# Adapted mixture-of-experts LoRA layer on one core: the transposes of W and of batch 1's inputs moved from TensorE to VectorE

## The chip, the cores and the metric

One core of a Trainium2 chip runs the whole layer as one program. The metric is the device time of one execution in microseconds (us). Below, PE is TensorE, DVE is VectorE, ACT is ScalarE, POOL is GpSimd and SP is SyncE, which here only starts transfers.

## The reference

Eight batches of 512 tokens with 2048 features go through two residual LoRA steps. The first has one adapter per batch, the second a dense matrix W and eight experts of rank 16, of which each token uses the best two:

```python
# x (8, 512, 2048), A0 (64, 2048, 16), B0 (64, 16, 2048)
x = x + einsum('bnr,bor->bno', einsum('bni,bri->bnr', x, B0[id_b]), A0[id_b])
# W (2048, 2048), Wr (8, 2048), A (8, 16, 2048), B (8, 2048, 16)
base = einsum('btd,od->bto', x, W)
logits = einsum('btd,ed->bte', x, Wr) + 5.0 * one_hot(language_b)
weights = softmax(top2(logits)); gates = scatter(weights)
lora = einsum('bter,bte,eor->bto', einsum('btd,erd->bter', x, A), gates, B)
x = x + base + 2.0 * lora
```

The residual is folded into W: the kernel adds the identity to W's diagonal blocks.

## The kernel before, in words

All matrix work is in float32, and each product is made of three rounded ones: high by high, high by low, low by high (`three_products`, lines 810 to 813; `pair_hi` on ACT writes the high part of a tile of W or of its sums, `pair_lo` on DVE the low part).

**Batch 0** multiplies plainly. Its time is cut into 36 slots (`SLOTS0`): in the four blocks of 512 output features there are eight slots with a tile of W each, 24 products of 512 columns per slot, and a ninth (8, 17, 26, 35) with the 12 products of the gated LoRA part. **Batches 1 to 7** use a scheme of seven products in place of eight on half-size blocks (Strassen, Winograd's form), with 60 slots each of 12 products. Their weight operands are W's blocks and four sums of these. Batch 0 makes them while it multiplies and stores them in DRAM (`t_scr`), and every later batch loads them from there, 512 KB a slot (`pair_load`, L780).

**How W comes in.** W lies in DRAM with the output features as rows, but the products want the input features on the partitions. For each of the 32 tiles g, SP loads 512 KB to `raw` (`first_load`, L674, four transfers, runs of 512 bytes). DVE adds the identity to the 8 diagonal tiles (`add_identity`, L684, two instructions each). PE turns the tile over in two halves of four 128x128 transposes into bank 7 (`w_transpose`, L698), and ACT copies each half out (`w_keep`, L709). Then DVE makes the four sums (`w_sums`, L733 to L738) and POOL stores blocks and sums (`w_store` L747 and L748, `w_sums_store` L753).

**How x comes in.** For batches 0 and 1, SP loads 512 KB tiles in runs of 2 KB, and PE turns them in units of four transposes (`x_transpose`, L322); ACT and DVE copy batch 0's out, ACT alone batch 1's (`x_keep`, L341). For batches 2 to 7, the 128-byte runs are scattered on load so that 32x32 blocks lie where DVE's own block-wise transpose gives the whole result (`x_turn`, L268), and PE has no part in it; a tile takes 16 transfers (L289). ACT and DVE split each unit (`x_hi`, `x_lo`), PE multiplies it with the small matrices (`aux_products`, L387 and L389), and later `delta` (L541) and `adapt` (L548) add the first adapter's part.

**What sets the order.** Each engine runs an order written out by hand (`pe_main`, `dve_main`, and so on), in which the work for coming slots stands between that of the present one; semaphores tie the engines. In slot i of batch 0, PE transposes tile i+3, ACT and DVE split tile i+2, and SP starts the load of tile i+5, which waits until tile i+3 has been turned (`raw` has two places for tiles as they come and two for turned ones). `wh` and `wl` have three places, so the split of tile i+2 waits for the products of slot i-1:

```python
            if g >= RING:
                wait_used(e, g - RING)
            e.copy(pair_split(wh, g), pair_source(g)).then_inc(c_wh, 1)
```

The sums go to `tst` or to part of `ost`, and the next sums to the same place wait until the store from there has landed (`d_ts`). At the end of a block, `first_evacuate` (L847, L849) copies the four PSUM banks to `ost`, and the first product of the next block waits for it. Before slot 0 there is a start (`pe_start`, `dve_start`) that turns batch 0's x, the adapters and experts, and tiles 0 to 2.

## Time and profile before

| | us |
|---|---|
| median of 3 runs | 1611.66 |
| lowest, highest | 1604.69, 1611.77 |
| the profiled execution | 1614.29 |
| its span, first to last instruction | 1612.5 |
| PE, DVE, ACT, POOL busy in it | 1580.2, 1179.3, 754.0, 74.1 |

A profile shows one execution. An engine's busy time counts its instructions alone; matmuls overlap, so the time from the start of one to the start of the next tells what it costs, not its duration. The DMA share is the busy time of packets over that of 16 engines; since packets overlap, it can read over 1.

### The profile page before, as it was taken

What the parts mean: (1) busy time and instruction counts of PE and PEld (TensorE: products, weight loads), DVE (VectorE), ACT (ScalarE), POOL (GpSimd) and SP (SyncE); (2) the same over time, 40 slices, a digit from 0 to 9 for tenths busy, and PEclk for the clock granted to TensorE, in tenths of its full rate; (3) what the DMA queues carried; (4) which work ended last, traced back from release to release, by engine and by line L of the source; (5) the groups of instructions that cost most, each with busy time, mean ns of one, the idle gap of its engine ahead of it and who ended that gap; (6) DMA issues with size and microseconds to landing.
All of it is one profiled execution on the core that took longest, in us unless ns stands there. A gap on an engine that the chain in (4) does not pass through costs nothing.

```text
span 1612.5 us, 21199 instructions
## 1 busy us (share of the span) xinstructions
PE 1580.2 (98%) x7766; PEld 1335.1 (83%) x7766; DVE 1179.3 (73%) x1603; ACT 754.0 (47%) x988; POOL 74.1 (5%) x117
## 2 busy tenths in 40 slices
PE   8899999999999999999999999999999999999998
PEld 7777887788888888888888888888888888888887
DVE  5774444687778876887778976888769877787665
ACT  5544433255444544455444554445544544445443
POOL 1222222100000000000000000000000000000000
PEclk9999999999999999999999999999999999999999
DMA  9888687768797886779876797878977797565664
GB/s 250 245 248 248 190 246 211 194 196 229 200 226 232 219 208 206 233 216 237 204 220 222 216 231 188 233 228 225 215 204 230 219 229 198 200 235 201 208 222 157
DMA packets 375658, 351.45 MB, mean 218 GB/s; under 512 B 250554, under 2 KB 294890, under 8 KB 374634
## 3 DMA queue, kind: packets, MB, share of 16 engines
q1 hardware_dynamic: 366290, 318.62, 71.6%
q0 software_dynamic: 8992, 30.94, 6.0%
q8 instruction: 62, 1.02, 0.3%
q10 hardware_dynamic: 272, 0.52, 0.1%
q14 instruction: 42, 0.34, 0.1%
HBM read 280.75 MB, written 68.82 MB: 217 GB/s over the span
## 4 chain that ended last, share of the span: by engine, by line
PE 93%; DMA 4%; DVE 1%; SPq 1%; issue 1%; ACT 1%; POOL 0%; ACTq 0%; DVEq 0%
PE pb L811 27%; PE pb L812 27%; PE pb L813 27%; PE pb L387 4%; PE pb L389 3%; PE pb L541 2%; PE pb L698 1%; DMA raw<-in_L_cond_W_dram 1%; DMA b0n<-in_L_cond_B_dram 1%; DMA ost<-in_L_cond_B_dram 1%; DMA t_scr<-raw 1%; PE pb L322 0%; SPq L674 0%; DMA ost<-in_x_dram 0%; SPq L1356 0%
## 5 line engine op out<-in xcount | busy, mean ns | idle before, releaser
L807 DVE TENSOR_TENSOR wl<-raw,wh 128x1024 fp32r<-128x1024 f32 (+1 forms) x456 | 555.0, 1217 | 349.3 <-ACT wh L803 349.0
L803 ACT CAST wh<-raw 128x1024 fp32r<-128x1024 f32 (+1 forms) x456 | 477.1, 1046 | 680.1 <-PE pb L813 680.0
L811 PE MATMUL pb<-wh,sh 128*128 128x512 f32 x1568 | 612.8, 391 | 0.5 <-DVE ost L849 0.5
L812 PE MATMUL pb<-wl,sh 128*128 128x512 f32 x1568 | 611.5, 390 | 0.0
L813 PE MATMUL pb<-wh,sl 128*128 128x512 f32 x1568 | 611.1, 390 | 0.0
L813 PEld LDWEIGHTS pb<-wh,sl 128*128 128x128 f32 x1568 | 294.3, 188 | 62.8
L811 PEld LDWEIGHTS pb<-wh,sh 128*128 128x128 f32 x1568 | 294.6, 188 | 56.1 <-DVE wl L807 0.9
L812 PEld LDWEIGHTS pb<-wl,sh 128*128 128x128 f32 x1568 | 294.6, 188 | 55.0
L387 PE MATMUL pb<-awb,xah 128*128 128x304 f32 x512 | 139.2, 305 | 0.0
L389 PE MATMUL pb<-awb,xal 128*128 128x256 f32 x512 | 135.0, 281 | 0.0
L811 PE MATMUL pb<-wh,xh 128*128 128x512 f32 x256 | 106.1, 415 | 0.8 <-DVE ost L849 0.8
L813 PE MATMUL pb<-wh,xl 128*128 128x512 f32 x256 | 102.0, 398 | 0.0
L812 PE MATMUL pb<-wl,xh 128*128 128x512 f32 x256 | 101.8, 398 | 0.0
L389 PEld LDWEIGHTS pb<-awb,xal 128*128 128x128 f32 x512 | 96.9, 189 | 4.2
L387 PEld LDWEIGHTS pb<-awb,xah 128*128 128x128 f32 x512 | 96.7, 189 | 4.4
L620 DVE TENSOR_TENSOR sl<-pool_a,sh 128x512 fp32r<-128x512 f32 x120 | 82.0, 684 | 0.0
L709 ACT COPY raw<-pb 128x512 f32<-128x512 f32 x64 | 37.7, 589 | 77.1 <-PE pb L698 74.7
L615 ACT CAST sh<-pool_a 128x512 fp32r<-128x512 f32 x120 | 73.5, 613 | 0.0
L548 DVE TENSOR_TENSOR pool_a<-pool_a,pb 128x512 f32<-128x512 f32 x88 | 58.8, 680 | 7.9 <-PE pb L541 7.9
L364 DVE TENSOR_TENSOR xal<-pool_a,xah 128x512 fp32r<-128x512 f32 x88 | 60.2, 685 | 5.8 <-ACT xah L359 5.6
L359 ACT CAST xah<-pool_a 128x512 fp32r<-128x512 f32 x88 | 54.7, 623 | 14.0 <-DVE pool_a L268 13.8
L813 PEld LDWEIGHTS pb<-wh,xl 128*128 128x128 f32 x256 | 48.9, 191 | 10.9
(151 smaller groups left out, 1335.0 us busy)
## 6 DMA issues: line engine op xcount, KB each, us to landing
raw<-t_scr SPq DMA_DIRECT2D x392, 512.0 KB, 4.2
xst<-in_x_dram SPq DMA_DIRECT2D x768, 32.0 KB, 3.9
raw<-in_L_cond_W_dram SPq DMA_DIRECT2D x124, 128.0 KB, 4.0
raw<-bt_scr SPq DMA_DIRECT2D x28, 512.0 KB, 3.6
out_dram<-ost SPq DMA_DIRECT2D x28, 512.0 KB, 4.2
out_dram<-u SPq DMA_DIRECT2D x28, 512.0 KB, 3.4
t_scr<-tst POOLq DMA_DIRECT2D x17, 512.0 KB, 5.2
t_scr<-raw POOLq DMA_DIRECT2D x32, 256.0 KB, 4.8
```

The costliest lines, as they stand in the source:

```text
L359: e.copy(x_high(n, u).rearrange("p k t -> p (k t)"), two(n, q, kp)).then_inc(c_xh, 1)
L364: e.tensor_tensor(out=x_low(n, u).rearrange("p k t -> p (k t)"), in0=two(n, q, kp), in1=x_high(n, u).rearrange("p k t -> p (k t)").bitcast ...
L387: e.matmul(pb[:, aux_bank(n, u // 8) + t, 0:2 * AW], x_high(n, u)[:, k, toks], cols[:, 0:2 * AW], start=u % 8 == 0 and k == 0, stop=False)
L389: last = e.matmul(pb[:, aux_bank(n, u // 8) + t, 0:LOW], x_low(n, u)[:, k, toks], cols[:, 0:LOW], start=False, stop=u % 8 == 7 and k == 1)
L548: e.tensor_tensor(out=two(n, q, kp), in0=two(n, q, kp), in1=pb[:, delta_bank(n, u), :], op=ALU.add)\
L615: e.copy(sh[:, h % SR, :, :].rearrange("p k t -> p (k t)"), two(b, SUM_QUARTER[product], kp)).then_inc(c_sph, 1)
L620: e.tensor_tensor(out=sl[:, h % SR, :, :].rearrange("p k t -> p (k t)"), in0=two(b, SUM_QUARTER[product], kp), in1=sh[:, h % SR, :, :].rea ...
L803: e.copy(pair_split(wh, g), pair_source(g)).then_inc(c_wh, 1)
L807: e.tensor_tensor(out=pair_split(wl, g), in0=pair_source(g), in1=pair_split(wh, g).bitcast(f32), op=ALU.subtract).then_inc(c_wl, 1)
L811: e.matmul(o, h, wh[:, g % RING, k, :], start=start, stop=False)
L812: e.matmul(o, h, wl[:, g % RING, k, :], start=False, stop=False)
L813: return e.matmul(o, l, wh[:, g % RING, k, :], start=False, stop=stop)
```

## The change

The outputs of the seven-product scheme are no longer the left and the right half of the features: within each block of 512 output features, the first and the second 256 are the two halves, and for the inputs the even and the odd features. A run in DRAM is then 64 floats (256 bytes) for x of batches 1 to 7 and for W. Both are scattered on load and turned by DVE with instructions of 128x512 whose input has a step of two elements:

```diff
-        x_b = x.rearrange("b (h v j) (c k a i) -> b h c k a j v i", h=2, j=32, c=4, k=4, a=4)
+        x_b = x.rearrange("b (h v j) (c k a n) -> b h c k a j v n", h=2, j=32, c=4, k=2, a=4)
...
-            e.transpose(two(n, q, kp).rearrange("p (k v j) -> p v k j", k=2, v=8),
-                        x_block(m)[:, :, u % 2 * 2:u % 2 * 2 + 2, :]).then_inc(c_xc, 1)
+            e.transpose(two(n, q, kp).rearrange("p (g j) -> p g j", g=16),
+                        x_block(m).rearrange("p (g i h) -> p h g i", g=16, h=2)[:, u % 2, :, :]).then_inc(c_xc, 1)
...
         def x_unit(u):
-            return u // 4, u % 4
+            return u // 8 * 2 + u % 2, u // 2 % 4
...
-        raw_w = W.rearrange("(w c j p) (h k n) -> c k w p j h n", w=2, c=4, j=2, p=P, h=2, k=HK)
+        raw_w = W.rearrange("(c g j) (k a n) -> c k a j g n", c=4, g=16, k=HK, a=4)
...
+        def w_turn(e, g):
...
+            diagonal = k // 2 == c
+            raw_landed(e, g)
+            if w >= 2:
+                e.wait_ge(c_wl, g - 2 - (g % 9 < 2) + 1)
+                wait_sums(e, w - 2)
                 e.wait_ge(d_bs[w % 2], 32 * (w // 2))
...
+            for h in range(2):
+                e.transpose(w_kept(g)[:, h, :].rearrange("p (g j) -> p g j", g=16),
+                            w_raw(g).rearrange("p (g i h) -> p h g i", g=16, h=2)[:, h, :, :])\
+                 .then_inc(c_id if diagonal else c_wc, 1)
+            if diagonal:
+                for h in range(2):
+                    e.wait_ge(c_id, 4 * c + 2 * (k % 2) + h + 1)
+                    block = w_kept(g)[:, h, k % 2 * HT:(k % 2 + 1) * HT].rearrange("p (n h) -> p h n", h=2)[:, h, :]
+                    e.tensor_tensor(out=block, in0=block, in1=ident[:, :], op=ALU.add).then_inc(c_wc, 1)
```

`w_transpose`, `w_keep`, `add_identity`, `x_keep` and the calls of `x_transpose` for batch 1 are gone, and with them the bank between PE and ACT. The adapters, Wr and A are read with the same step of two in the start. From the fourth tile of W on, two of the four sums are POOL's:

```diff
+        def w_sum_3(e, g):
+            b11, b12, b21, b22 = w_blocks(g)
+            e.wait_ge(c_wc, 2 * w_number(g) + 2)
+            wait_sum_place(e, g)
+            e.tensor_tensor(out=w_sum(g)[:, 3, :], in0=b12, in1=b11, op=ALU.subtract).then_inc(c_tp, 1)
+
+        def w_sum_2(e, g):
+            b11, b12, b21, b22 = w_blocks(g)
+            e.wait_ge(c_t, 2 * w_number(g) + 8)
+            e.tensor_tensor(out=w_sum(g)[:, 2, :], in0=b21, in1=w_sum(g)[:, 0, :], op=ALU.subtract).then_inc(c_tp, 1)
...
             for i in range(SLOTS0):
-                if i + 2 < SLOTS0 and (i + 2) % 9 != 8:
+                sums = i + 2 < SLOTS0 and (i + 2) % 9 != 8
+                if sums and i:
+                    w_sum_3(e, i + 2)
+                if i + 3 < SLOTS0 and (i + 3) % 9 != 8:
+                    w_store(e, i + 3)
+                if sums and i:
+                    w_sum_2(e, i + 2)
+                if sums:
                     w_sums_store(e, i + 2)
```

The results of batches 1 to 7 go out in runs of 1 KB, two transfers of 256 KB in place of one of 512 KB. In the later batches, x's units stand at slightly other slots, and what follows them (`bx`, `aux_adapted`, `delta`, `adapt`, the gates) three slots later:

```diff
-                e.dma_start(out_v[b, 0, :, :, c * CW:(c + 1) * CW], ost[:, 2 * c:2 * c + 2, :]).then_inc(d_ost[c], 16)
+                for t in range(2):
+                    e.dma_start(out_v[b, 0, t, 0, :, 2 * c:2 * c + 2, :],
+                                ost[:, 2 * c + t, :].rearrange("p (c n) -> p c n", c=2)).then_inc(d_ost[c], 16)
...
-        X_AT = {4 * (u // 2) + 4 + u % 2: u for u in range(16)}
+
+        X_AT = {at: u for u, at in enumerate((4, 5, 8, 9, 12, 13, 16, 17, 21, 24, 25, 28, 29, 32, 33, 36))}
...
-                        if 41 <= i < 57:
-                            delta(e, n, i - 41)
+                        if i >= 44:
+                            delta(e, n, i - 44)
```

On PE, at the border of two slots of batch 0 (`pb` are the PSUM banks, `xst` and `raw` the tiles of x and W as they came), there stood before:

```order
L812 MATMUL pb<-wl,xh 128x512
L813 MATMUL pb<-wh,xl 128x512
L322 MATMUL pb<-ident,xst 128x128 x4
L698 MATMUL pb<-ident,raw 128x128 x4
L811 MATMUL pb<-wh,xh 128x512
```

and stands now:

```order
L809 MATMUL pb<-wl,xh 128x512
L810 MATMUL pb<-wh,xl 128x512
L808 MATMUL pb<-wh,xh 128x512
```

Both rows of transposes went. On DVE, slot 11 of batch 0 was the split of tile 13 (`wl`), the four sums of tile 13 (`tst`) and the low part of a unit of x (`xal`):

```order
L807 TENSOR_TENSOR wl<-raw,wh 128x1024
L733 TENSOR_TENSOR tst<-raw 128x256
L734 TENSOR_TENSOR tst<-raw 128x256
L736 TENSOR_TENSOR tst<-tst,raw 128x256
L738 TENSOR_TENSOR tst<-raw,tst 128x256
L364 TENSOR_TENSOR xal<-pool_a,xah 128x512
```

and is now:

```order
L270 STREAM_TRANSPOSE pool_a<-xst 128x512
L804 TENSOR_TENSOR wl<-raw,wh 128x1024
L674 STREAM_TRANSPOSE raw<-raw 128x512 x2
L349 TENSOR_TENSOR xal<-pool_a,xah 128x512
L717 TENSOR_TENSOR tst<-raw 128x256
L721 TENSOR_TENSOR tst<-tst,raw 128x256
```

Three transposes came, two sums went, and the sums stand behind the turning of the next tile. In the start, DVE made the sums of tile 0 right after `st48`, ahead of the first `adapt`s (`pool_a`):

```order
L414 TENSOR_TENSOR st48<-aux,st48 128x4x16
L733 TENSOR_TENSOR tst<-raw 128x256
L734 TENSOR_TENSOR tst<-raw 128x256
L736 TENSOR_TENSOR tst<-tst,raw 128x256
L738 TENSOR_TENSOR tst<-raw,tst 128x256
L548 TENSOR_TENSOR pool_a<-pool_a,pb 128x512 x2
```

Now tile 1 is turned there, and the sums of tile 0 come after the split of tile 1, directly ahead of tile 2's turning and tile 1's sums:

```order
L804 TENSOR_TENSOR wl<-raw,wh 128x1024
L1138 TENSOR_TENSOR late<-late 128x136
L717 TENSOR_TENSOR tst<-raw 128x256
L719 TENSOR_TENSOR tst<-raw 128x256
L721 TENSOR_TENSOR tst<-tst,raw 128x256
L724 TENSOR_TENSOR tst<-raw,tst 128x256
L674 STREAM_TRANSPOSE raw<-wrn 128x512 x2
L717 TENSOR_TENSOR tst<-raw 128x256
```

## Rows read from the trace of the kernel before

**Rows 1.** the page, busy time of each engine

```profile
PE 1580.2 (98%) x7766; PEld 1335.1 (83%) x7766; DVE 1179.3 (73%) x1603; ACT 754.0 (47%) x988; POOL 74.1 (5%) x117
```

**Rows 2.** windows: us, busy (count) of PE PEld DVE ACT POOL, clock, DMA share, GB/s

```profile
63.08:131.66 68.58, 63.90 (x326) 52.38 (x325) 45.78 (x104) 30.66 (x47) 18.69 (x28) 0.97 0.78 228
131.66:199.24 67.58, 66.46 (x368) 57.08 (x369) 29.22 (x54) 28.20 (x48) 16.81 (x26) 1.00 0.75 216
199.24:265.61 66.37, 65.62 (x360) 56.15 (x361) 29.26 (x57) 25.58 (x44) 14.94 (x24) 1.00 0.74 213
265.61:329.47 63.86, 57.60 (x279) 47.98 (x278) 37.17 (x87) 18.43 (x28) 12.13 (x19) 0.95 0.76 208
329.47:1600.00 1270.53, 1270.53 (x6042) 1068.78 (x6043) 996.72 (x1238) 614.31 (x764) 0.00 (x0) 1.00 0.78 218
```

**Rows 3.** PE's order of time in slot 14 of batch 0 (start, us)

```profile
176.52 0.60 PE L698 MATMUL pb<-ident,raw 128*128 128x128 f32 x4
176.88 0.48 PE L811 MATMUL pb<-wh,xh 128*128 128x512 f32 x1
177.19 0.40 PE L812 MATMUL pb<-wl,xh 128*128 128x512 f32 x1
177.42 0.39 PE L813 MATMUL pb<-wh,xl 128*128 128x512 f32 x1
```

**Rows 4.** PE's order of time at its two long stops

```profile
62.31 1.12 PE L698 MATMUL pb<-ident,wrn 128*128 128x128 f32 x4 [6.42 <-ACT raw L709]
...
284.68 1.11 PE L698 MATMUL pb<-ident,raw 128*128 128x128 f32 x4 [5.75 <-DMA raw<-in_L_cond_W_dram]
286.02 0.63 PE L812 MATMUL pb<-wl,xh 128*128 128x512 f32 x1
286.45 0.63 PE L813 MATMUL pb<-wh,xl 128*128 128x512 f32 x1
```

**Rows 5.** DVE's groups (xcount | busy, mean ns | idle before, releaser)

```profile
L807 DVE TENSOR_TENSOR wl<-raw,wh 128x1024 fp32r<-128x1024 f32 x452 | 552.2, 1222 | 342.7 <-ACT wh L803 342.4
...
L364 DVE TENSOR_TENSOR xal<-pool_a,xah 128x512 fp32r<-128x512 f32 x88 | 60.2, 685 | 5.8 <-ACT xah L359 5.6
L268 DVE STREAM_TRANSPOSE pool_a<-xst 128x512 f32<-128x512 f32 x56 | 39.4, 704 | 0.0
...
L684 DVE TENSOR_TENSOR raw<-raw,ident 128x128 f32<-128x128 f32 x16 | 3.9, 287 | 15.5 <-DMA raw<-in_L_cond_W_dram 15.5
```

**Rows 6.** ACT's groups: two copies of 512 elements

```profile
L709 ACT COPY raw<-pb 128x512 f32<-128x512 f32 x64 | 37.7, 589 | 77.1 <-PE pb L698 74.7 <-DMA t_scr<-raw 2.5
...
L1075 ACT COPY a0t<-pb 128x512 f32<-128x512 f32 x4 | 4.3, 1079 | 0.7 <-PE pb L1070 0.7
```

**Rows 7.** POOL's and DVE's order of time around 50 us

```profile
50.46 1.62 POOL L1304 COPY xst<-ost 128x256 f32<-128x256 f32 x4 [18.47 <-DMA ost<-in_L_cond_B_dram]
...
51.20 0.62 DVE L733 TENSOR_TENSOR tst<-raw 128x256 f32<-128x256 f32 x1
...
64.06 0.43 DVE L733 TENSOR_TENSOR tst<-raw 128x256 f32<-128x256 f32 x1 [3.75 <-ACT raw L709]
```

**Rows 8.** the page, DMA issues, last number: us to landing

```profile
t_scr<-tst POOLq DMA_DIRECT2D x17, 512.0 KB, 5.2
```

**Rows 9.** DMA packets of 1440 to 1560, 460 to 580, 131.6 to 199.2 us

```profile
DMA packets 7429, 25.25 MB, mean 210 GB/s; under 512 B 768, under 2 KB 768, under 8 KB 7422
...
q1 hardware_dynamic: 7422, 25.16, 61.4%
...
DMA packets 32606, 27.49 MB, mean 229 GB/s; under 512 B 25695, under 2 KB 25695, under 8 KB 32599
...
q1 hardware_dynamic: 32599, 27.39, 83.6%
...
DMA packets 13093, 14.56 MB, mean 215 GB/s; under 512 B 1040, under 2 KB 10512, under 8 KB 13087
```

**Rows 10.** a window in which the DMA share reads over 1

```profile
205.00:210.00 5.00, 5.00 (x28) 4.22 (x27) 2.31 (x5) 2.54 (x4) 0.89 (x2) 1.00 1.08 316
```

More of the change, by code:

```diff
@@ L328, in x_keep_act @@
             e.wait_ge(c_tr, u + 1)
-            e.copy(two(0, q, kp), pb[:, x_bank(0, u), :]).then_inc(c_x0[0], 1)
+            e.copy(two(0, q, kp), pb[:, x_bank(u), :]).then_inc(c_x0[0], 1)
         def x_keep_dve(e, u):
@@ L671, in first_load @@
                      .then_inc(landed, 16)
-                else:
-                    for h in range(2):
-                        e.dma_start(w_raw(g)[:, 2 * w:2 * w + 2, h, :], raw_w[c, k, w, :, :, h, :])\
-                         .then_inc(landed, 16)
-        def add_identity(e, g):
-            c, k = divmod(g, 9)
-            if k // 2 != c:
-                return
-            raw_landed(e, g)
-            for h in range(2):
-                block = w_raw(g)[:, 2 * h + k % 2, h, :]
-                e.tensor_tensor(out=block, in0=block, in1=ident[:, :], op=ALU.add).then_inc(c_id, 1)
@@ L686, in w_transpose @@
[L686 removed]
+            else:
+                for a in range(4):
+                    e.dma_start(w_raw(g)[32 * a:32 * a + 32, :].rearrange("p (g n) -> p g n", g=16), raw_w[c, k, a])\
+                     .then_inc(landed, 16)
+        def w_turn(e, g):
             c, k = divmod(g, 9)
             w = w_number(g)
[L689 to L699 removed]
@@ L996, in a_transpose @@
             for k in range(4):
-                last = e.transpose(pb[:, m, k * P:(k + 1) * P], an[:, (4 * m + k) * P:(4 * m + k + 1) * P], ident[:, :])
+                last = e.transpose(pb[:, m, k * P:(k + 1) * P], tile_of(an[:, :], a_tiles(m).start + k), ident[:, :])
             last.then_inc(c_ap, 1)
@@ L1272, in dve_start @@
             bx_lo(e, 0)
-            w_sums(e, 0)
+            w_turn(e, 1)
             for u in range(2):
@@ L1284, in dve_start @@
             g_lo(e)
+            w_sums(e, 0)
+            w_turn(e, 2)
             w_sums(e, 1)
[L1286 to L1287 removed]
         def pool_start(e):
@@ L1376, in pe_main @@
             for i in range(SLOTS0):
-                more = i + 3 < SLOTS0 and (i + 3) % 9 != 8
                 if i == 4:
@@ L1442, in act_main @@
             for i in range(SLOTS0):
-                more = i + 3 < SLOTS0 and (i + 3) % 9 != 8
-                if i < 2:
-                    w_keep(e, i + 2, 1)
                 if i == 6:
@@ L1474, in act_main @@
                         sum_hi(e, 1, 0, kp)
-                if i and more:
-                    w_keep(e, i + 3, 1)
                 if i in (17, 25):
@@ L1527, in dve_main @@
                         adapt(e, 1, u)
+                if i + 3 < SLOTS0 and (i + 3) % 9 != 8:
+                    w_turn(e, i + 3)
+                if 9 <= i < 25:
+                    x_lo(e, 1, i - 9)
                 if i + 2 < SLOTS0 and (i + 2) % 9 != 8:
```

285 lines of the change are left out of this document (122 added, 163 removed).

## The prediction, made before the changed kernel had run

> **What bounds the kernel now.** I read the engines' busy time first: PE is busy for 1580.2 of 1612.5 us, DVE for 1179.3 [rows 1]. The average hides two kinds of time, so next I read windows. Batches 1 to 7 (329.47 to 1600 us) have PE busy for every microsecond of 1270.53 at full clock [rows 2]. The change takes no PE instruction out of them, so nothing can be won there; it can only be lost. Batch 0 takes four windows of 68.58, 67.58, 66.37 and 63.86 us (slots 0 to 8, 9 to 17, 18 to 26, 27 to 35), with PE idle for 4.68, 1.12, 0.75 and 6.26 us of them. So in the two middle windows PE has nearly no gaps, and what it does less is won unless something else takes over; in the first and the last, waits count too. PE's own order of time gives the price of a transpose group and the two long stops [rows 3, 4]. DVE's groups give what the new work costs there [rows 5], and the DMA packets tell how much room the transfers have [rows 9].
>
> **PE: transposes removed.** A group of four starts 0.36 us before the next product, and this product takes 0.31 us to its successor where 0.23 is the rule: 0.36 + 0.08 = 0.44 us [rows 3]. The 64 half tiles of W and 16 units of batch 1's x are 80 groups, 35.2 us. Six groups lie ahead of the first product at 63.08 us, where other things bound; 74 remain. In slots 9 to 17 there are 16 of W and 9 of x, 25 x 0.44 = 11.0 us; in slots 18 to 26 16 and 7, 10.1 us; in slots 27 to 35 10 of W, 4.4 us; the other 16, 7.0 us, are in slots 0 to 8.
>
> **PE: waits removed.** At 278.9 us PE stops for 5.75 us because the transposes of a tile stand in its queue and the tile has not come [rows 4]. Now DVE waits for the tile, and PE needs it two slots later, some 10 us of slack. I let this stop go, and with it the slow clock behind it: products 0.43 us apart in place of 0.23 [rows 4], and a mean clock of 0.95 in that window [rows 2], which is 5% of 63.86, 3 us, of which the stop itself holds a part; I take 2. The other stop, 6.42 us at 55.9 us [rows 4], waited for ACT's copy of tile 2, which waited for a store. This chain goes too, but the start has others (below).
>
> **ACT** loses 80 copies of 0.589 us [rows 6], 47 us of an engine that is busy for 754.0 [rows 1]. Nothing waits for ACT for long in batch 0's middle, so I take nothing for it.
>
> **DVE: what comes.** A tile costs two transposes. The nearest row is the same instruction without the step of two, 0.704 us [rows 5]. From below nothing speaks for less. From above, ACT's copy of 512 elements costs 0.589 us packed and 1.079 us with a stepped output [rows 6], 1.83 times; by this a transpose would be 1.29 us. I take 0.70, the nearest row: the same operation, engine and size. In slots 9 to 24 DVE then has per slot: `pair_lo` 1.22, three transposes 2.11, the low part of x 0.69 and two sums of 0.43 [rows 5, 7], 4.9 us, and in two tiles of eight twice 0.29 more for the identity. The 67.58 us of slots 9 to 17 are eight slots and a half one, 7.95 us each; with three groups less, PE's slot lasts 6.6. DVE fits, with 1.7 us over, and its split of a tile is needed two slots later. So this is hidden, as long as a transpose stays under some 1.1 us.
>
> **POOL's sums.** Two of 256 elements per slot, on an engine busy for 74.1 us in all [rows 1]; hidden behind everything, except that they may slow DVE. The trace shows that: DVE's first sum of 256 elements took 0.62 us while POOL copied, and 0.43 us otherwise [rows 7]. So a DVE sum or split beside each of POOL's loses 0.2 us, 0.4 per slot, inside the 1.7 us. The Trainium skill, SBUF — State Buffer, section "Who interferes with whom", says that a VectorE instruction with two SBUF inputs contends with a GpSimd one that reads SBUF, and that the second blocks until the first ends. By that rule the loss could be up to the length of POOL's own instruction, which no row shows; from POOL's copy (1.62 us for four, [rows 7]) I bound it at twice 0.8 per slot for a form with two inputs, 1.6 us, which would just use up the room.
>
> **DMA: smaller packets.** Between 1440 and 1560 us (no x is loaded) q1 moves 25.16 MB in 7422 packets with 61.4% of 16 engines, 1179 engine-us or 46.9 us per MB. Between 460 and 580 us it moves 27.39 MB in 32599 packets with 83.6%, 1605 engine-us. The 2.23 MB more are worth 105, so 321 engine-us are for 25177 small packets more: 12.8 ns each [rows 9]. A tile of W had 1024 packets and gets 2048; a tile of batch 1's x had 256 and gets 2048. For slots 9 to 17 (8.5 tiles of W, 3.5 of x) that is 15000 packets, 192 engine-us, on top of 0.75 x 16 x 67.58 = 811 [rows 2]: 1003, or 62.7 us at a share of 1. The share can read over 1: 1.08 at 316 GB/s [rows 10], by which it is 58. PE alone would need 67.58 - 11.0 = 56.6. So in this window DMA and PE come out nearly even, and I take 59.5, 8 us less than before. For slots 18 to 26 (8 of W, 2.5 of x) it is 786 + 162 = 948, 59.3 or 54.9 us, against 56.3 of PE: I take 58, 8.4 less. In slots 27 to 35, 7 tiles of W add 7168 packets, but the first two tiles of batch 2's x lose 4096, and 777 + 39 = 816 engine-us is 51 us: no bound. The bounds of a packet's price are nothing (packets of 256 bytes pack better than those of 128) and 25.6 ns (one costs as much as two of 128). The Trainium skill, DMA: Bandwidth & Descriptors, section Specifications, asks for at least 512 bytes for the full rate and says that smaller transfers do read-modify-write; W's runs go from just that size to half of it, so it speaks against this change. What it would do here is the second rival.
>
> **The last quarter.** 4.4 us of transposes, 5.75 of the stop and 2 of the clock are 12.2; but there DVE has three `adapt`s a slot, the top-two chain and a turning, and the evacuation behind slot 26 now stands behind a turning of 1.4 us. I give 2 back: 10 less.
>
> **The start and slots 0 to 8.** Slots 0 to 6 are DVE's: `adapt` and split of two units, the split of the tile, now also its turning (1.4) for two sums less (0.86), so 0.5 us a slot more. Further, the sums of tile 0 come later, and those of tile 1 wait for their store to land, 5.2 us [rows 8], in front of tile 2's split, where PE will stop in slot 1. On the other side, the stop of 6.42 us goes, slot 0 can begin some 5 us earlier, and the waits of transposes for tiles 10 and 11 go. Adding the DVE instructions up one by one I come to a start of slot 9 at 127.7 us in place of 131.66: 4 less, give or take 5. This is the softest term.
>
> **Later batches.** x's units and `delta` move by up to three slots, in an order in which PE has no gap; x loads have half the packets (98304 less, 1258 engine-us, or 79 us of share over 1270); results go out in 112 transfers for 56. PE bounds: 0. If this cover went, one DVE round late would show as PE idle in a window that has none now. The last store starts as two transfers: +0.3.
>
> **Sum:** -4 - 8 - 8.4 - 10 + 0.3 = -30. The profiled execution took 1614.29 us (span 1612.5 and 1.8 around it) and would take 1584. The median of the runs, 1611.66, is 2.6 below it, so the forecast of the median is 1582 us.
>
> **The rivals.**
> - PE alone bounds: packets of 256 bytes cost little more than their bytes. Then the middle windows give 11.0 and 10.1 and the last 12.2: -37, 1575 us. For it speaks that PE is gapless there; against it the share of 0.75 before any packet was added. 0.15.
> - DMA bounds at the full 12.8 ns and a share of 1: middle windows 62.7 and 59.3, -4.9 and -7.1, last -8, start -4: -24, 1588. 0.21. This is also the skill's rule in its mild form.
> - The same at 25.6 ns: 811 + 384 = 1195 engine-us are 74.7 us in place of 67.6, the second window 786 + 325 are 69.4 (+3), the start loses its 4, the last keeps -8: about +2, 1614, no change. 0.05.
> - The softest term fails: in slots 0 to 6 DVE's chain and the wait for the store cost 8 instead of winning 4, all else as forecast: -18, 1594. 0.07.
> - **Slower:** DVE becomes the bound of batch 0. At 1.29 us a transpose, DVE's slot is 6.7, with 0.4 for POOL 7.1: under the old 7.95, but slots 0 to 6 lose 12 and the last quarter is even; the whole comes out near zero. Each 0.1 us more costs 80 x 0.1 = 8 us. At 1.6 us it is +25, 1637. It decides from 1.3 us. For it speaks ACT's stepped row; against it that this is another engine, and output, not input. 0.04.
>
> **How the numbers follow.** The forecast case has 0.48. Half a percent, 8 us, is about what a measurement of this kernel can tell from no change. Faster by more than that are the forecast, the first, the second and the fourth rival: 0.48 + 0.15 + 0.21 + 0.07 = 0.91; no change 0.05; slower 0.04. The range goes from 1571 (the first rival with a start that gives 4 more) to 1596 (the fourth, and the second with a start that gives nothing), which leaves out the third and the fifth and some of the edges.
>
> **What would show it.** Right: no transposes of W on PE; slots 10 to 16 between 6.5 and 6.9 us apart; the stop before slot 29 gone; `w_turn` transposes near 0.70 us; batches 1 to 7 unchanged with PE gapless; the DMA share in the middle windows from 0.9 to 1.05. Wrong: transposes over 1 us, DVE busy for over 90% of a middle window, PE waiting for `wl` while DVE waits for W, or slot 9 starting after 131.66 us.

## The result, and the profile after

| | before | after |
|---|---|---|
| median, 15 runs each on one chip | 1609.90 | 1603.86 |
| lowest, highest | 1602.12, 1611.77 | 1601.00, 1606.35 |
| profiled execution | 1614.29 | 1606.35 |
| its span | 1612.5 | 1604.6 |

The ratio is 0.9966, 95% interval [0.9955, 0.9978]: faster, by 6 us and not by 30. That is less than the half percent (8 us) which the prediction took for what can be told from no change, though the interval leaves 1 out, and it lies outside the range of 1571 to 1596 us.

The stretches of the profiled executions in us, cut at the first product of a slot (read off PE's order of time), each with the part of the forecast's sum that spoke of it:

| stretch | before | after | forecast | came |
|---|---|---|---|---|
| start of slot 9 | 131.66 | 141.51 | -4 | **+9.85** |
| slots 9 to 26 | 133.95 | 122.61 | -16.4 | -11.34 |
| slots 27 to 35 | 63.86 | 55.18 | -10 | -8.68 |
| batches 1 to 7 | 1278.43 | 1280.52 | 0 | +2.09 |
| behind the last product | 4.6 | 4.8 | +0.3 | +0.2 |

The page of the changed kernel, busy time of each engine, beside [rows 1]:

```profile
PE 1556.7 (97%) x7446; PEld 1308.1 (82%) x7446; DVE 1221.7 (76%) x1625; ACT 713.9 (44%) x908; POOL 126.2 (8%) x176
```

Its windows by block, beside [rows 2] (us, busy of PE, PEld, DVE, ACT, POOL, clock, DMA share, GB/s):

```profile
58.01:141.51 83.50, 57.67 (x252) 46.10 (x253) 60.65 (x117) 24.10 (x33) 35.16 (x45) 0.87 0.89 215
141.51:203.00 61.49, 57.71 (x269) 48.51 (x269) 41.23 (x65) 15.51 (x22) 28.75 (x39) 0.94 0.96 229
203.00:264.12 61.12, 58.34 (x272) 48.84 (x273) 38.81 (x64) 14.55 (x22) 28.68 (x40) 0.95 0.93 235
264.12:319.30 55.18, 54.32 (x240) 44.52 (x241) 43.43 (x85) 12.87 (x18) 22.84 (x30) 0.94 0.92 238
319.30:1599.80 1280.50, 1280.46 (x6076) 1074.34 (x6076) 999.93 (x1239) 615.23 (x764) 0.00 (x0) 1.00 0.72 216
```

PE's work shrank as the transposes went (57.67 us in the first block in place of 63.90), but the first block grew by 15 us: PE is idle for 26 of its 83.50 us, DVE is busy for 60.65 in place of 45.78, and the granted clock is 0.87 in place of 0.97. (Slot 0 starts 5.07 us earlier, at 58.01, so that slot 9 is later by 9.85 only.) What PE waits for, whole run (us in total, times, longest):

```profile
PE pb L808 <- DVE ost L846: 14.9, 4, 9.9
PE pb L1147 <- ACT bt L1152: 9.9, 1, 9.9
PE pb L408 <- DVE st L399: 5.1, 2, 3.0
PE pb L526 <- DVE pool_a L533: 4.0, 3, 2.7
```

The two longest are the stops to read. **The stop in slot 1.** DVE's order of time, changed kernel:

```profile
63.17 0.42 DVE L724 TENSOR_TENSOR tst<-raw,tst 128x256 f32<-128x256 f32 x1
63.80 1.30 DVE L674 STREAM_TRANSPOSE raw<-wrn 128x512 f32<-128x512 f32 x2 [0.20 <-DVE tst L724]
68.70 0.42 DVE L717 TENSOR_TENSOR tst<-raw 128x256 f32<-128x256 f32 x1 [3.60 <-DMA t_scr<-tst]
...
71.31 1.28 DVE L533 TENSOR_TENSOR pool_a<-pool_a,pb 128x512 f32<-128x512 f32 x2
72.67 1.29 DVE L553 TENSOR_TENSOR xl<-pool_a,xh 128x512 fp32r<-128x512 f32 x2
73.88 1.30 DVE L674 STREAM_TRANSPOSE raw<-raw 128x512 f32<-128x512 f32 x2
```

ACT's, and PE's, behind it:

```profile
75.22 1.04 ACT L800 CAST wh<-raw 128x1024 fp32r<-128x1024 f32 x1 [1.98 <-DVE raw L674]
76.17 1.03 ACT L1152 COPY bt<-pb 128x512 f32<-128x512 f32 x1
```

```profile
77.25 1.11 PE L1147 MATMUL pb<-ident,xst 128*128 128x128 f32 x4 [9.86 <-ACT bt L1152]
...
79.01 0.63 PE L808 MATMUL pb<-wh,xh 128*128 128x512 f32 x1
79.44 0.63 PE L809 MATMUL pb<-wl,xh 128*128 128x512 f32 x1
```

Read backwards: PE stops for a copy on ACT; this stands behind the high part of tile 3, which waits for tile 3's turning at 73.88, and that is late because DVE, in order, had waited 3.60 us for the store of tile 0's sums to leave `tst`. None of the waiting engines was short of work to do; a queue held it. And behind the stop products are 0.43 us apart: the granted clock is 0.50 from 79 to 82 us, 1.00 before the stop (66 to 68 us).

**The stop ahead of slot 9.** POOL's order of time, then DVE's and PE's:

```profile
127.43 0.73 POOL L744 DMA_DIRECT2D t_scr<-raw  x1 [4.74 <-DVE raw L674]
...
128.75 1.80 POOL L735 TENSOR_TENSOR ost<-raw,ost 128x256 f32<-128x256 f32 x1
131.09 0.78 POOL L750 DMA_DIRECT2D t_scr<-ost  x1 [0.54 <-POOL ost L735]
```

```profile
125.82 1.30 DVE L674 STREAM_TRANSPOSE raw<-raw 128x512 f32<-128x512 f32 x2 [1.78 <-DMA raw<-in_L_cond_W_dram]
...
133.35 1.30 DVE L674 STREAM_TRANSPOSE raw<-raw 128x512 f32<-128x512 f32 x2 [3.40 <-DMA raw<-in_L_cond_W_dram]
...
140.67 1.29 DVE L846 COPY ost<-pb 128x512 f32<-128x512 f32 x2 [4.85 <-DMA t_scr<-ost]
```

```profile
141.51 0.76 PE L808 MATMUL pb<-wh,xh 128*128 128x512 f32 x1 [9.87 <-DVE ost L846]
142.07 0.63 PE L809 MATMUL pb<-wl,xh 128*128 128x512 f32 x1
```

PE may not write the banks again until they are copied to `ost`; the copy waits until the sums that lie in `ost` have been stored; POOL issued this store at 131.09 only, since the store of tile 10, which had to be turned first, stands ahead in its queue and its own sum took 1.80 us; and it landed 9.5 us later, against a median of 5.5 for `tst`. Smaller stops of this kind stand ahead of slots 18 (3.8 us) and 27 (0.7 us).

### The profile page after: what moved, and what is told of

The parts are those of the page before. It is cut to its first block, busy times and chain, and to the rows that moved or that the text cites. A ratio compares the mean times of both kernels' runs of the same rounds, so it can differ in the third digit from the quotient of the medians.

```text
span 1604.6 us, 20300 instructions
## 1 busy us (share of the span) xinstructions
PE 1556.7 (97%) x7446; PEld 1308.1 (82%) x7446; DVE 1221.7 (76%) x1625; ACT 713.9 (44%) x908; POOL 126.2 (8%) x176
## 4 chain that ended last, share of the span: by engine, by line
PE 88%; DVE 5%; DMA 4%; ACT 1%; issue 1%; SPq 1%; POOL 0%; DVEq 0%; ACTq 0%; POOLq 0%
PE pb L808 26%; PE pb L809 26%; PE pb L810 26%; PE pb L372 4%; PE pb L374 3%; PE pb L526 2%; DMA xst<-in_x_dram 1%; DVE raw L674 1%; DMA t_scr<-ost 1%; DVE wl L804 1%; DMA b0n<-in_L_cond_B_dram 1%; ACT wh L800 1%; DVE pool_a L533 1%; SPq L659 0%; DMA an<-in_L_cond_A_dram 0%
## 5 line engine op out<-in xcount | busy, mean ns | idle before, releaser
L808 PEld LDWEIGHTS pb<-wh,xh 128*128 128x128 f32 x256 | 50.7, 198 | 27.3 <-issue 16.1
L270 DVE STREAM_TRANSPOSE pool_a<-xst 128x512 f32<-128x512 f32 x72 | 50.9, 706 | 14.0 <-DMA xst<-in_x_dram 13.9
```

The lines of the kernel that those rows point to most:

```text
L808: e.matmul(o, h, wh[:, g % RING, k, :], start=start, stop=False)
```

## The experiments

All ratios are to the kernel before, run beside each in five rounds; intervals are 95%. Gains of an edit are told as differences of medians. They are uncertain by some 2 us: the kernel before measured 1611.0 us beside e1, e2, e6 and e7 and 1609.9 beside the changed kernel, so that by the ratios each of these gains about 2 us more. For an edit's mechanism the traces decide, but each shows one execution: in those of the kernels built on the changed one, slot 0 starts between 56.62 and 58.55 us, so a stretch counted from slot 0 says more than a time. A slot's length is the distance from its first product to the next slot's.

| run | edit, on the changed kernel unless said | median | ratio |
|---|---|---|---|
| after | | 1603.86 | 0.9966 [0.9955, 0.9978] |
| e1_pool_order | sums' store ahead of W's | 1600.43 | 0.9932 [0.9912, 0.9951] |
| e2_sums0_early | tile 0's sums early | 1602.07 | 0.9938 [0.9920, 0.9957] |
| e6_ost_swap | evacuation swapped | 1603.97 | 0.9953 [0.9936, 0.9970] |
| e7_three | e1 + e2 + e6 + x load order | 1597.44 | 0.9918 [0.9899, 0.9937] |
| e3_sums_dve | no sums on POOL | 1595.09 | 0.9915 [0.9901, 0.9928] |
| e5_shift_before | before + the shift of three slots | 1613.07 | 1.0015 [1.0000, 1.0029] |
| e8_x_whole | e7 + x tiles loaded whole | 1592.12 | 0.9898 [0.9883, 0.9913] |
| e9_bt_first | e7 + ACT's order | 1598.74 | 0.9943 [0.9929, 0.9958] |
| e12_pool_idle_sums | e3 + unused sums on POOL | 1601.17 | 0.9944 [0.9926, 0.9963] |
| e10_all_dve | e3 + e1 + e2 + both x edits | 1592.58 | 0.9895 [0.9877, 0.9913] |
| e13_all_dve_swap | e10 + e6 | 1590.36 | **0.9883 [0.9863, 0.9903]** |
| e14_half_turn | e13, tiles half turned | 1589.14 | 0.9857 [0.9840, 0.9873] |

**POOL's order.** Move W's store back behind the sums':

```diff
-                if i + 3 < SLOTS0 and (i + 3) % 9 != 8:
-                    w_store(e, i + 3)
                 if sums and i:
                     w_sum_2(e, i + 2)
                 if sums:
                     w_sums_store(e, i + 2)
+                if i + 3 < SLOTS0 and (i + 3) % 9 != 8:
+                    w_store(e, i + 3)
```

> The changed kernel with one edit on GpSimd: in a slot of batch 0 the store of W's plain blocks (w_store of tile i+3, which waits for the transposes of that tile) stands again behind the last sum and the store of the sums of tile i+2, as before the change. Theory Q (queue order: the store of tile 9's sums was issued at 131.09 us, behind that wait, and landed at 140.58; the first evacuation waited for it): slot 9 starts near 134 instead of 141.51, TensorE's 9.9 us wait for the evacuation is 2 to 4 us, and the time is 6 to 10 us below the changed kernel's 1603.9, 1594 to 1598 (ratio to the kernel before 0.990 to 0.993). Rival D (the transfers themselves are late, since 256-byte packets fill the DMA engines, share 0.89 to 0.96 in batch 0): the store still lands 9 us after its issue and slot 9 starts within 2 us of 141.5, 1602 to 1604 (ratio 0.996). Rival P (POOL has no room before its sum is ready, so the order does not matter): as D, with the store of the sums issued at 129 or later.

The time fell by 3.4 us, about half of the least that the theory wanted; slot 9 starts at 138.34, not near 134. The store went out at 129.12 in place of 131.09, and landed only at 137.5, 8.4 us later. So the queue's order is part of it, and the long landing, rival D's, the other part. Rival P was not far off either: POOL's sum could not begin before DVE's was ready, at 127.86 in place of 128.75, and 1.1 of the 2.0 us that the store gained are this sum's own length, 0.72 us in place of 1.80.

**Tile 0's sums** before tile 1's turning, in `dve_start`:

```diff
             bx_lo(e, 0)
+            w_sums(e, 0)
             w_turn(e, 1)
...
             g_lo(e)
-            w_sums(e, 0)
             w_turn(e, 2)
```

> The changed kernel with one edit on VectorE: the sums of W's tile 0 are made right behind the first half of bx, as before the change, ahead of tile 1's transposes instead of behind them. Theory V (VectorE's queue: its first sum of tile 1 waited 3.60 us, to 68.70, for the store of tile 0's sums to leave the staging tile; this wait went on through pair_lo, adapt, w_turn(3), ScalarE's pair_hi(3) and its copy of Bt to TensorE's 9.86 us stop at 67.4 to 77.3): slot 2 starts at 77 to 80 instead of 83.74 and the time is 4 to 7 us below 1603.9, 1597 to 1600 (ratio 0.993 to 0.994). Rival W (what is late is W's tile 3 or the transposes themselves, 0.7 us each, and the wait for the store only fills that time): slot 2 at 82 to 84, time within 1.5 us of 1603.9. Rival S (what slot 1 gains is lost at slot 8, whose stop ends with the store of tile 9's sums, whatever came earlier): slot 2 early, slot 9 again at 140 to 141.5, time within 2 us of 1603.9.

Slot 2 starts at 81.84, 1.9 us earlier, and the median is 1.8 lower. Most of PE's stop (8.5 of 9.9 us) stays, but this does not clear the wait for the store: the edit did not take it away. POOL's and DVE's order of time in this run:

```profile
56.97 0.75 POOL L750 DMA_DIRECT2D t_scr<-tst  x1
...
67.07 0.43 DVE L717 TENSOR_TENSOR tst<-raw 128x256 f32<-128x256 f32 x1 [4.02 <-DMA t_scr<-tst]
```

Tile 0's sums were made by 51.9 us, but POOL issued their store at 56.97, behind its own copies, and DVE still waited 4.02 us for it (3.60 before): it had landed 10.1 us after its issue, in the changed kernel 4.8 us after (63.90 to 68.70). The landing moved by 1.6 us, and about that is what the run gained. Were the wait gone, DVE could turn tile 3 some 4 us earlier (an estimate from this row); the other half of the stop would remain. No run took the wait away. Slot 9 kept the gain (139.48), against the third theory.

**The evacuation** to the halves of `ost` that hold no sums first:

```diff
+            o = (t + 2) % 4
             if c:
-                e.wait_ge(d_ost[t // 2], 32 * c)
-            if t < 2:
+                e.wait_ge(d_ost[o // 2], 32 * c)
+            if o < 2:
...
-                e.copy(ost[:, t, :], pb[:, t, :]).then_inc(c_eva, 1)
+                e.copy(ost[:, o, :], pb[:, t, :]).then_inc(c_eva, 1)
```

> The changed kernel with one edit in the evacuations of batch 0: banks 0 and 1 go to the two output tiles that hold no sums of W, banks 2 and 3 to the two that also stage the sums, so that the first two evacuations need not wait for the store of the sums. Theory E (the stops ahead of slots 9, 18 and 27, 9.9, 3.8 and about 1 us, are waits for the staging tile and not for the evacuation's work): TensorE's waits for the evacuation are under 2 us in all, the half clock behind them is gone or shorter (2.8 us each), and the time is 10 to 18 us below 1603.9, 1586 to 1594 (ratio 0.985 to 0.990). Rival H (VectorE's and ScalarE's queues are themselves behind, since VectorE waits for x and W there; the evacuation would be late without the staging tile): the stop ahead of slot 9 is 4 us or more, and the time 1598 to 1602 (ratio 0.993 to 0.995).

A miss: the same median within 0.1 us, outside both ranges (2 us less by the ratios). Slot 9 starts at 137.27 in place of 141.51, but takes 11.65 us in place of 8.29, as PE now stops inside it for the second pair of banks, whose copies wait 4.0 and 8.4 us for the same store. The wait was moved behind two banks, not removed. Later the profile is ahead all the same, at slot 32 by 5.0 us (291.89 for 296.93), since slot 27 takes 5.96 us in place of 8.82; but in slot 32 PE waits 2.1 us for an `adapt` of DVE, and slots 32 and 33 give 3.4 us back (8.86 and 7.77 for 7.05 and 6.21).

**The three together, and the second x load** of batch 1 a slot later:

```diff
-                if i in (4, 5):
-                    x_load(e, 1, i - 4)
+                if i in (4, 6):
+                    x_load(e, 1, i // 2 - 2)
```

> The changed kernel with four edits together: the store of W's plain blocks behind the sums on GpSimd, the sums of tile 0 early on VectorE, the second load of batch 1's x issued behind first_load(11) instead of ahead of it, and banks 0 and 1 evacuated to the tiles that hold no sums. Theory (the changed kernel lost what it saves on TensorE in waits of three queues): slot 2 at 77 to 80, slot 9 at 124 to 128, slot 18 at 185 to 190, slot 27 at 246 to 250, batch 1 from 302 to 307, and 1583 to 1590 (ratio 0.983 to 0.988). Rival (the DMA engines, at a share of 0.93 to 0.96 in the middle of batch 0, have nothing left to give, so that whatever starts earlier waits longer for its W and x): slots 9 to 36 take 5 us or more longer than the changed kernel's 177.8 us, and the time is 1593 to 1600.

Up to slot 9 the theory's numbers came, or nearly (79.53, 128.42), and behind it, in part, the rival's: slots 9 to 35 took 181.39 us, 3.6 more than the changed kernel's 177.79, where the rival wanted 5. The time is inside the rival's range. Ahead of slot 18 PE waits 6.5 us. DVE there, in this run:

```profile
185.99 0.42 DVE L721 TENSOR_TENSOR ost<-ost,raw 128x256 f32<-128x256 f32 x1
191.08 0.71 DVE L270 STREAM_TRANSPOSE pool_a<-xst 128x512 f32<-128x512 f32 x1 [4.67 <-DMA xst<-in_x_dram]
191.72 1.18 DVE L804 TENSOR_TENSOR wl<-raw,wh 128x1024 fp32r<-128x1024 f32 x1
...
195.78 1.28 DVE L847 COPY ost<-pb 128x512 f32<-128x512 f32 x2
```

The turning of x, first in the slot, waits 4.67 us for its tile, and the evacuation stands behind it.

**All sums on DVE**; POOL only stores:

```diff
-            if w < 3:
+            if True:
                 e.tensor_tensor(out=t[:, 3, :], in0=b12, in1=b11, op=ALU.subtract).then_inc(c_t, 1)
...
-                if sums and i:
-                    w_sum_3(e, i + 2)
...
-                if sums and i:
-                    w_sum_2(e, i + 2)
```

> The changed kernel with all four sums of W on VectorE and none on GpSimd, so that GpSimd only issues stores again. VectorE gets 0.85 us a slot more (two sums at 0.42), but its operations are no longer prolonged by GpSimd's (wl at 1.55 to 1.76 us instead of 1.22 in slots 3 to 8, xl's pair at 2.04 to 2.37 instead of 1.29), and the store of the sums no longer waits for GpSimd's two sums (0.7 to 1.8 us each) behind W's store. Theory G (the split of the sums is what costs slots 3 to 9): wl back at 1.22, slot 9 starts 4 to 7 us earlier than 141.51, and the time is 1597 to 1600 (ratio to before 0.992 to 0.994). Rival V (VectorE's total work decides, 60.7 of 83.5 us up to slot 9): slot 9 at 141 or later and 1603 to 1608 (ratio 0.996 to 0.999). Slots 10 to 17, where VectorE was busy 29.3 of 45.5 us, should stay at 6.5 us either way.

The largest gain of one edit, 8.8 us (8.2 by the ratios), more than the theory asked; slot 9 starts at 135.00. DVE's order of time with the splits beside POOL's sums in the changed kernel, then the same in this run:

```profile
92.48 1.55 DVE L804 TENSOR_TENSOR wl<-raw,wh 128x1024 fp32r<-128x1024 f32 x1 [0.35 <-ACT wh L800]
...
95.32 2.37 DVE L553 TENSOR_TENSOR xl<-pool_a,xh 128x512 fp32r<-128x512 f32 x2
...
100.72 1.76 DVE L804 TENSOR_TENSOR wl<-raw,wh 128x1024 fp32r<-128x1024 f32 x1
```

```profile
91.74 1.22 DVE L802 TENSOR_TENSOR wl<-raw,wh 128x1024 fp32r<-128x1024 f32 x1
...
94.24 1.29 DVE L553 TENSOR_TENSOR xl<-pool_a,xh 128x512 fp32r<-128x512 f32 x2
...
99.24 1.22 DVE L802 TENSOR_TENSOR wl<-raw,wh 128x1024 fp32r<-128x1024 f32 x1
```

Over slots 2 to 5 the changed kernel's splits of W and x lasted some 3 us longer than this run's. Slots 10 to 16 stayed at 6.5 us, with twice the sums on DVE.

**The same work on POOL, for nobody**: e3_sums_dve with two subtractions a slot on a spare tile.

```diff
+            for half in range(2):
+                e.wait_ge(c_tp, 2 * n + half)
+                e.tensor_tensor(out=spare[:, :], in0=spare[:, :], in1=spare[:, :], op=ALU.subtract)\
+                 .then_inc(c_tp, 1)
```

> The form of e3_sums_dve (all four sums of W on VectorE, 1595.1 us), and GpSimd makes in every slot of batch 0, behind the slot's stores, two 128x256 subtractions on a tile of its own that nobody reads: GpSimd's two sums of the changed kernel again as work, without anyone waiting for their result and without W's stores behind them in the slot. It measures what GpSimd's use of the shared port costs VectorE. Theory C (contention is most of what e3_sums_dve won back, 8.8 us): wl and xl of slots 3 to 8 are prolonged again (wl 1.4 to 1.8 us instead of 1.22), slot 9 starts 3 us or more after e3_sums_dve's 135.99, and the time is 1598 to 1602. Rival O (what e3_sums_dve won is the order: the sums' store no longer waits behind GpSimd's sums and W's store): slot 9 within 1.5 us of 136, and the time 1594 to 1597.

(The 135.99 there is the third product of e3's slot 9; the first, as everywhere in this text, is at 135.00.) The time rose by 6.1 us to 1601.17 (4.7 by the ratios), and the fastest run of this kernel (1596.67) is above the slowest of e3 (1595.61). The time is theory C's, its signs are not: slot 9 came only 1.4 us later or, counted from slot 0, 2.7, and in slots 3 to 8 a single split of a tile was prolonged, at 98.60 us, to 1.73. DVE's splits of tiles and of x between 64 and 305 us, this run, then e3_sums_dve:

```profile
L803 DVE TENSOR_TENSOR wl<-raw,wh 128x1024 fp32r<-128x1024 f32 x31 | 40.6, 1308 | 17.7 <-ACT wh L799 17.7
...
L350 DVE TENSOR_TENSOR xal<-pool_a,xah 128x512 fp32r<-128x512 f32 x16 | 11.4, 710 | 0.0
```

```profile
L802 DVE TENSOR_TENSOR wl<-raw,wh 128x1024 fp32r<-128x1024 f32 x31 | 37.7, 1217 | 23.7 <-ACT wh L798 23.3
...
L349 DVE TENSOR_TENSOR xal<-pool_a,xah 128x512 fp32r<-128x512 f32 x16 | 10.6, 660 | 0.0
```

So work on POOL that nobody waits for costs 5 to 6 of the 8.8 us. How it does is open. DVE's instructions in these two rows are 3.7 us longer, but most of that lies in slots 10 to 16 and 19 to 25, which take 6.5 us in both runs. Counted from slot 0 the profile loses 4.8 us by slot 18, and the two largest parts stand where DVE waits for a load: for W's tile 11 5.0 us, in e3 2.4, and for a tile of x ahead of slot 18 4.2, in e3 2.5. Whether POOL's work made these loads late, or only this execution did, was not tried. What remains of the 8.8, some 3 us, is of the size of e1's 3.4.

**The shift of later batches**, alone in the kernel before; `bx`, `aux_adapted` and the gates move likewise:

```diff
-                        if 41 <= i < 57:
-                            delta(e, n, i - 41)
+                        if i >= 44:
+                            delta(e, n, i - 44)
```

> The kernel before with one part of the change alone: in batches 1 to 7 bx, the adapted aux sum, the deltas and the gates of the next batch stand three slots later. The changed kernel's batches 1 to 7 took 2.3 us more than before's (1285.3 against 1283.0 us, 0.3 us a batch) with TensorE gapless in both; the deltas' matmuls were 0.124 us apart instead of 0.121. Theory L (the shift costs it): batches 1 to 7 take 1285 us, the time is 1 to 3 us above the kernel before (ratio 1.0005 to 1.002). Rival M (it comes with the x transposes as 256-byte packets or the output's stores, that is with other traffic on SBUF, or with the layout of the products' operands): batches 1 to 7 take 1283.0 within 0.3 us, and no difference can be measured.

Its batches 1 to 7 took 1280.5 us, as the changed kernel's, in place of 1278.4, PE gapless; this window is the evidence, since the ratio's interval just reaches 1:

```profile
321.03:1601.50 1280.47, 1280.44 (x6076) 1074.50 (x6076) 999.14 (x1239) 615.15 (x764) 0.00 (x0) 1.00 0.79 216
```

All 12 other profiles of kernels with the shift say the same: from the first product of batch 1 to the last of the kernel they take 1279.85 to 1280.25 us, this one 1280.12, and before 1278.04. (The absolute lengths in the expectation, 1283.0 and 1285.3, run to the end of the span; the difference is the same.) The run says one more thing: with the same program up to batch 1 as before, it starts slot 0 at 58.83 us and slot 9 at 125.53, where the profiled execution of before had 63.08 and 131.66. Part of what that profile showed in its start was that execution's own.

**x loaded whole**, on e7:

```diff
-                if 11 <= i < 23:
-                    x_load(e, 1, (i - 7) // 2, (0, 1) if i % 2 else (2, 3))
+                if 11 <= i < 23 and i % 2:
+                    x_load(e, 1, (i - 7) // 2)
```

> The four edits of e7_three and a fifth: batch 1's input tiles 2 to 7 are each loaded by eight transfers at once in every second slot of batch 0, instead of four in one slot and four in the next, which SyncE issues only after the W tile in between. Theory X (latency of x decides slots 15 and 17 of e7_three: VectorE's x transposes, first in its slot, waited 2.9, 4.7 and 6.0 us for their tile, and with them W's transposes and the evacuation ahead of slot 18): these waits are under 1 us, slot 15 takes 6.5 instead of 8.38 and slot 17 takes 6.6 to 8 instead of 10.41, and the time is 3 to 6 us below e7_three's 1597.4, 1591 to 1594. Rival B (the DMA engines' throughput decides; what x gains, W loses): VectorE waits for W instead, slots 9 to 27 still take 127 to 128 us, and the time is within 1.5 us of 1597.4.

Theory X: 5.3 us less (3.2 by the ratios), slot 14 (the expectation miscounts it as 15) at 6.49 us in place of 8.38, slot 17 at 8.01 in place of 10.41. The waits for x fell to 1.9 and 2.4 us, if not under 1. A transfer's place in SP's queue, not the DMA engines' capacity, was what x lacked.

**ACT's order**, on e7:

```diff
-                pair_hi(e, i + 2)
                 if i in (1, 2):
                     bt_copy(e, 2 * i - 2)
+                    bt_copy(e, 2 * i - 1)
+                pair_hi(e, i + 2)
```

> The four edits of e7_three and, instead of a fifth on the loads, one on ScalarE: in slots 1 and 2 the copies of Bt's transposes stand ahead of pair_hi of the W tile two slots on. Theory A (TensorE's stop in slot 1, still 7.3 us in e7_three, is a wait for a copy that stands on ScalarE behind pair_hi(3), and this one waits for VectorE's transposes of tile 3 to 71.6 us; nothing that slot 2's products need is late): the stop in slot 1 is under 1.5 us, slot 2 starts at 71 to 74 instead of 79.53, and the time is 4 to 7 us below e7_three's 1597.4, 1590 to 1593. Rival V (VectorE's own queue, busy without a gap from 65 to 80 us, is what slots 3 to 5 wait for): slot 2 early but slot 5 at 99 to 101 as in e7_three (100.79), and the time within 1.5 us of 1597.4.

The rival, and worse: PE's stop is 5.3 us in place of 7.3 and slot 2 starts 1.1 us earlier, but slot 3 takes 8.68 in place of 6.33 us, slot 5 starts at 102.75, and the time is 1.3 us above e7's. DVE's queue was the limit behind ACT's. (Slot 17 was longer too, 12.00 us: DVE could turn its tile of x at 193.41 us only, in e7 at 191.08; why the tile came later is open.)

**Together, sums on DVE:**

> The form of e3_sums_dve with four of the edits tried before: on GpSimd the sums' store ahead of W's store, the sums of tile 0 early on VectorE, batch 1's second input tile loaded behind first_load(11), and its tiles 2 to 7 loaded whole in every second slot. If the gains are of different waits and add up (e3_sums_dve -8.8, e1 -3.4, of which e3 holds part, e2 -1.8, the whole loads -5.3 against the changed kernel or its combination): slot 2 at 79, slot 9 at 127 to 130, slot 18 at 188 to 191, batch 1 from 301 to 304, and 1586 to 1590 (ratio 0.985 to 0.987). Rival (slots 1 to 8 are bound by VectorE's total work, 50 of 62 us, and its four sums cost more there than the contention did): slot 9 at 131 or later and the time 1590 to 1594, no better than e8_x_whole's 1592.1.

The rival's numbers: slot 9 at 132.45, no better than e8. Its reason, that DVE's total work bounds there, is at most a part: ahead of slot 9 DVE stands idle for 3.34 us.

```profile
131.61 1.29 DVE L844 COPY ost<-pb 128x512 f32<-128x512 f32 x2 [3.34 <-DMA t_scr<-ost]
```

The sums' store was issued at 123.78 and landed 7.8 us later, and this kernel lacks the one edit of e8 that lets two banks go ahead of it.

> As e10_all_dve, and banks 0 and 1 evacuated to the output tiles that hold no sums. Theory E (the last stops ahead of slots 9 and 18 are waits for the staging tile): 2 to 4 us below e10_all_dve. Rival H (the evacuation waits for VectorE's own queue, as e6_ost_swap, which won 0.1 us by itself, seemed to say): within 1 us of e10_all_dve, either way.

By the medians theory E, at its low edge: 2.2 us. But the intervals overlap, and in the profiles batch 0 takes 246.09 us from slot 0 in place of 246.80, so that most of the difference between them stands ahead of slot 0, which this edit does not touch; between E and H this is open. The traces do show what the edit does here: the store goes out at 123.97, in e6 at 132.24, the copies of the second pair of banks wait 2.2 and 4.6 us for it in place of 4.0 and 8.4, and slot 9 starts 65.49 us after slot 1 in place of 67.49. This is the best version that computes the whole layer, 1.2% below before and 13.5 us faster than the changed kernel. Its middle windows:

```profile
129.21:191.17 61.96, 56.84 (x268) 47.20 (x269) 44.72 (x81) 17.12 (x23) 16.55 (x26) 0.97 1.07 255
191.17:251.32 60.15, 57.54 (x273) 47.94 (x273) 42.53 (x80) 13.38 (x20) 15.91 (x24) 0.97 1.04 241
```

**Less turning**, on e13. This kernel leaves half of eight tiles of W unturned (the expectation says which), so its output is not the layer's; it only measures:

```diff
             for h in range(2):
+                n = 1 if h and 3 <= g <= 11 else 16
```

> As e13_all_dve_swap, the best so far (1590.4 us, slot 1 at 63.72 and slot 9 at 129.21), with one thing left out: of the two transposes of each of W's tiles 3 to 7 and 9 to 11 on VectorE the second turns 32 columns instead of 512, so that these tiles' second halves keep old values in the output's first batch and in what is stored of W. That takes some 0.6 us out of VectorE's work in each of slots 0 to 8, about 5 us in all, and changes no transfer and no wait. Theory V (up to slot 9 VectorE's own work is the limit, 49.7 us busy of 60.7 with TensorE at 47.7): slot 9 comes 3 to 5 us earlier after slot 1's start (60.5 to 62.5 us instead of 65.5), and the time is 3 to 5 us below 1590.4, 1585 to 1587.5. Rival L (the stops are latency: of transfers, and of hand-overs between the engines, with VectorE's 11 idle us as room): slot 9 within 1.5 us of 65.5 after slot 1, and the time within 1.5 us of 1590.4.

Between the theories: from slot 1 to slot 9 63.16 us in place of 65.49, 2.3 less for 4.2 taken (eight times 0.69 - 0.17). By these two executions DVE's work bounds about half of that stretch, latency the rest. The median is 1.2 us lower, 4.2 by the ratios, which leaves open how much of the 2.3 reaches the end; in the profiled execution slot 10 gave it back (10.62 us in place of 7.87).

## Why the prediction was wrong

**The step that failed** is the term "The start and slots 0 to 8", put at -4, give or take 5, and called the softest: it measured +9.85, 14 of the 22 us that are missing. Slot 0 did begin 5.1 us earlier, as said; slots 0 to 7 took 7.1 us more (70.63 for 63.54), slot 8 with the stop at its end 7.8 more (12.87 for 5.04). Its parts:
- "up one by one I come to a start of slot 9 at 127.7". The instructions' prices were right (transposes 0.686 and 0.706 us for 0.70). The sum counted work and one wait on DVE. That wait came no larger than foreseen: 3.6 us, the store landing 4.8 us after its issue. It left out what DVE's lateness does through the other queues: ACT's copy of Bt behind the high part of tile 3, with 9.9 us of PE standing still, and the half clock behind it (slot 1 took 19.36 us for 8.68). The text named "PE will stop in slot 1" and gave that stop no price.
- "hidden behind everything": POOL's sums. Without them the kernel is 8.8 us faster (e3), and 5 to 6 of these go to POOL's mere work, whoever waits for it (e12). I had allowed 0.4 us a slot "inside the 1.7 us" of room, which belongs to slots 9 to 24. In slots 0 to 6 there is no room. The Trainium skill's rule (SBUF — State Buffer, "Who interferes with whom"), that the second of the two blocks, agrees with the changed kernel's rows: 0.3 to 0.5 us on one split and 1.1 on a pair, and POOL's own sum stretched from 0.74 to 1.80. The 1.6 us a slot by which I had bounded it was twice the 0.8 that slots 2 to 5 show. How the rest of the 5 to 6 us comes about stays open.
- POOL's queue: the order shown in the diff moved W's store ahead of the sums' store, which the evacuation waits for. I looked at DVE's and PE's order, not at POOL's. 3.4 us (e1). And stores landed late at these places: 9.5 us after their issue at slot 9, 8.4 in e1, 10.1 for tile 0's in e2, where I had 5.2 [rows 8]. Why is open.

**Slots 9 to 26**, forecast -16.4, came at -11.3. Slots 10 to 16 came at 6.48 to 6.52 us, as the first rival had it: PE alone bounded, at a DMA share of 0.94, and in e13 of 1.07. The term's DMA working was wrong in kind. In those slots capacity did not bind; what cost were waits at the ends of blocks, where the evacuation stands behind DVE's waits for x (in e7 4.67 us, and less once x had a better place in SP's queue, e8) and for the sums' store. After the two stops slots 9 and 18 took 8.29 and 9.26 us, 1.8 and 2.8 more than their neighbours, with products at half clock. I had counted only work per slot and given the block's end nothing. The Trainium skill's rule against runs under 512 bytes (DMA: Bandwidth & Descriptors, Specifications) did not show as a bound here; W's landing went from 4.0 to 4.7 us.

**The last quarter** was forecast at -10 and came at -8.7: the stop before slot 29 is gone (5.74 us in place of 13.00), as foreseen; slot 32 takes 7.05 us, in e3 6.17, with a wait for DVE's `adapt` (0.25 us, in e6 2.1).

**Later batches**, put at 0 since "PE bounds": +2.1. PE stayed gapless, but a gapless PE can still be slower; e5 shows that the shift does it. In what way is open.

**The base.** The profiled execution was 4.4 us above the median of before that the comparison gave; e5 puts that in the start. There slot 9 starts at 125.53 us, against which the first term would read +16, and the stop of 6.42 us that I let go lasts 4.05.

Of the rivals the fourth, with the softest term at +8 and a chance of 0.07, was nearest, and half by luck: it had DVE's chain and the wait for the store in slots 0 to 6, which with slot 0's earlier start leave +2.0 at slot 8, but not the stop ahead of slot 9, which is the other 7.8; and the other terms came smaller. That slot 9 would start after 131.66 us, the sign for "wrong", came true.

## What to carry to other kernels

Where work moves from one in-order engine to another, add up its price on the new engine in the stretch where that engine has least room, and then walk every queue behind it: a wait at the head of one queue is passed on to engines that have nothing to do with it, and ends as an idle TensorE, with half the clock behind it. Look at the queues that only issue transfers as closely as at the arithmetic. Removing one stop often only shows the next: three single edits gave 3.4, 1.8 and 0 us by the medians, and all of them, with the sums back on VectorE and x loaded in one go, 13.5. And when an edit gives little, look first whether the wait that it aimed at is gone from the trace: in e2 it was longer than before.

## What the runs showed of the hardware

- Two-input work on GpSimd beside VectorE's: 128x1024 splits took 1.55 and 1.76 us in place of 1.22, GpSimd's own 128x256 subtraction 1.80 in place of 0.74. Sums that nobody used made the kernel 5 to 6 us slower (e12); in what way is open.
- A 128x512 transpose on VectorE costs the same with a stepped input (0.69 us) as without (0.70), though ACT's copy with a stepped output costs 1.83 times [rows 6].
- After the stops of 9.9, 9.9 and 3.8 us the granted clock was 0.50 (79 to 82, 141.5 to 147 and 203 to 206 us), and products were 0.43 us apart, 0.23 before and later.
- A 512 KB store of sums, whose median is 5.2 to 5.5 us from issue to landing in the changed kernel, took 9.5 us there ahead of slot 9, 8.4 in e1, 7.8 in e10 and 7.3 in e13, and 10.1 in e2 ahead of slot 2; why is open.
- TensorE without a gap can still take longer: seven batches with `delta` three slots later took 2.1 us more (1280.1 for 1278.0), within 0.3 us the same in all 13 profiles with the shift.
- Of two kernels with the same program up to batch 1, one execution each, slot 0 started at 58.83 and 63.08 us (e5 and before).
